# Two attention layers on one core: scores multiplied into the projection weights, F and G merged, the raw path moved behind the projection

## What is computed

```python
# layer 0: linear attention on qkv and on a depthwise 5x5 + grouped 1x1 copy of qkv
q, k, v = h @ wq.T, h @ wk.T, h @ wv.T
qkv = concat(q, k, v)                                  # 768 channels
pw = grouped_1x1(depthwise_5x5(qkv))                   # 768 channels
f = concat(qkv, pw).reshape(B, -1, 24, N)              # 32 "raw" and 32 "pw" heads
query, key_, value = relu(f[:, :, :8]), relu(f[:, :, 8:16]), f[:, :, 16:]
scores = einsum('bhdn,bhen->bhde', concat(value, 1), key_)
out = einsum('bhde,bhen->bhdn', scores, query)
out = out[:, :, :-1] / (out[:, :, -1:] + 1e-15)
x = batchnorm(conv1x1(out, proj)) + x
# layer 1: softmax attention over the 1024 pixels
norm = (x - mean(x)) / sqrt(var(x) + 1e-5)             # per channel
F, G = f_w @ norm + f_b, g_w @ norm + g_b
attention = softmax(F.T @ G)
x = o_w @ ((h_w @ x + h_b) @ attention.T) + o_b + x
```

## Time and profile before

| | us |
|---|---|
| median of 3 runs | 808.69 |
| lowest to highest | 807.97 to 808.84 |
| the profiled execution, its own time | 805.62 |
| its span, first to last instruction | 803.8 |
| busy: PE, DVE, POOL, ACT | 679.6, 597.0, 538.6, 505.5 |

### The profile page before, as it was taken

One profiled execution on the slowest core, in us unless ns is written; L12 is line 12 of the kernel. 1 busy time (PEld: TensorE's weight loads), 2 busy tenths in 40 slices (PEclk: granted clock), 3 DMA queues, 4 the chain that ended last, 5 costly groups with the idle time before them and its releaser, 6 DMA issues.

```text
span 803.8 us, 9440 instructions
## 1 busy us (share of the span) xinstructions
PE 679.6 (85%) x2892; PEld 457.7 (57%) x2892; DVE 597.0 (74%) x769; ACT 505.5 (63%) x731; POOL 538.6 (67%) x248
## 2 busy tenths in 40 slices
PE   4999988897788799898688799898688794888987
PEld 3744577655465477665465477665465462456743
DVE  6999599989757879989757879989757885443300
ACT  4944468865679768865679768865679754123730
POOL 3498968898778688997778688997778667000000
PEclk9999999999899999999899999999899997999999
DMA  5000020000000220000000220000000020000000
GB/s 200 2 0 1 0 106 1 1 1 0 1 1 1 79 79 0 0 0 0 0 0 0 79 79 0 0 0 0 0 0 0 27 79 0 1 0 1 1 26 26
DMA packets 4801, 15.93 MB, mean 20 GB/s; under 512 B 672, under 2 KB 928, under 8 KB 3744
## 3 DMA queue, kind: packets, MB, share of 16 engines
q1 hardware_dynamic: 4768, 15.56, 5.3%
HBM read 11.37 MB, written 4.19 MB: 19 GB/s over the span
## 4 chain that ended last, share of the span: by engine, by line
PE 48%; DVE 20%; ACT 13%; issue 13%; POOL 3%; DMA 1%; ACTq 0%; DVEq 0%; SPq 0%; POOLq 0%
PE ps L568 14%; DVE ps L937 9%; PE ps L494 7%; PE ps L544 6%; ACT prod L748 3%; PE ps L622 3%; PE ps L451 3%; PE ps L447 3%; PE ps L448 3%; POOL rows L1160 3%; PE ps L517 2%; ACT rows L862 2%; PE ps L504 2%; PE ps L559 2%; ACT kv L878 2%
## 5 line engine op out<-in xcount | busy, mean ns | idle before, releaser
L1160 POOL TENSOR_TENSOR conv<-conv,prod 128x930 f32<-128x930 f32 (+4 forms) x192 | 429.5, 2271 | 101.3 <-ACT prod L748 97.6
L937 DVE SCALAR_TENSOR_TENSOR ps<-raw,dw_sb,ps 128x960 f32<-128x960 f32 (+4 forms) x290 | 348.4, 1201 | 12.7 <-issue 4.8
L748 ACT ACTIVATE prod<-raw,dw_sb 128x930 f32<-128x930 f32 (+4 forms) x228 | 249.7, 1120 | 75.1 <-POOL conv L1160 62.4
L568 PE MATMUL ps<-kv,oc 128*128 128x512 f32 x256 | 111.6, 594 | 2.7 <-ACT kv L878 2.7
L1160 POOL TENSOR_TENSOR rows<-rows,prod 128x930 f32<-128x930 f32 (+4 forms) x36 | 83.2, 2310 | 14.9 <-ACT prod L748 12.3
L568 PEld LDWEIGHTS ps<-kv,oc 128*128 128x128 f32 x256 | 48.3, 190 | 61.4 <-issue 57.4
L1090 DVE TENSOR_REDUCE small<-ps 128x1 f32<-128x1024 f32 x32 | 39.2, 1225 | 58.1 <-PE ps L544 58.1
L559 PE MATMUL ps<-mask_sb,rows 128*128 128x128 f32 x256 | 37.6, 289 | 30.4 <-ACT kv L878 21.4
L517 PE MATMUL ps<-sd,rows 128*128 128x144 f32 x256 | 48.1, 322 | 17.7 <-DVE kv L999 13.7
L622 PE MATMUL ps<-oc,proj_sb 128*128 128x512 f32 x128 | 56.0, 595 | 1.4 <-ACT oc L774 0.8
L517 PEld LDWEIGHTS ps<-sd,rows 128*128 128x128 f32 x256 | 36.9, 201 | 31.0 <-DVE kv L999 23.5
(11 more groups left out here) (96 smaller groups left out, 1135.6 us busy)
## 6 DMA issues: line engine op xcount, KB each, us to landing
rows<-x_dram SPq DMA_DIRECT2D x4, 1024.0 KB, 4.9
x<-x_dram SPq DMA_DIRECT2D x4, 1024.0 KB, 4.8
out_dram<-x SPq DMA_DIRECT2D x8, 512.0 KB, 3.1
conv<-wqkv_dram SPq DMA_DIRECT2D x1, 768.0 KB, 4.4
conv<-fg_dram SPq DMA_DIRECT2D x1, 512.0 KB, 5.5
proj_sb<-proj_dram SPq DMA_DIRECT2D x1, 512.0 KB, 7.2
pw_sb<-pw_dram SPq DMA_DIRECT2D x1, 384.0 KB, 6.5
conv<-hw_dram SPq DMA_DIRECT2D x1, 256.0 KB, 5.7
```

The lines of the kernel that those rows point to most:

```text
L568: mm = pe.matmul(ps[:, 4 + c, :], ht[:, j, c * P:(c + 1) * P], pt[:, j, :], start=(j == 0), stop=(j == NB - 1))
L748: act.activation(dst, view, ACT.Copy, scale=weight(t, i)).then_inc(prod_ready, 1)
L937: return dve.scalar_tensor_tensor(dst, view, w, before, ALU.mult, ALU.add)
L1160: pool.tensor_tensor(total, total, product, ALU.add).then_inc(conv_pool, 1)
```

## The change

- **Scores into the weights.** The masked scores of both paths (`s_masked`) are transposed on TensorE (`score_transposes`, into `s_t`) and multiplied into the projection weights (`fused_weights`, into `mb`). The projection then takes `mb` and the scaled queries. The output matmuls, their eight-block division and the transposes back are gone.
- **q scaled by inverse denominators.** `denominators` multiplies q by `kd` (the key sums) with 32 output rows for each quarter of the pixels, so that all denominators of a path stand in one 128 x 256 block; VectorE adds epsilon and inverts it once; `spread_denominators` multiplies it by a 0/1 matrix with 32 contracted rows to copy each head's value to its channels; VectorE multiplies q by that, in four units of 512 pixels (`scaled_queries`). Before the second half of each pair of units TensorE waits for its own first half (`bc_part`).
- **F and G merged.** F.T @ G = norm.T (f_w.T g_w) norm and terms of the biases. `fg_hi` and `fg_lo` hold f_w.T g_w, made in the prologue; in a body only t = (merged weight) norm is made, four units in place of eight. The bias terms of a row come from 16 matmuls with one column each (`row`), and each row's maximum gets one more tiny VectorE operation with them.
- **Order.** Pointwise q comes straight behind the pw scores; the transposes of the next keys and values stand behind the denominators. The next image's q, its denominators, fused weights and scaling stand behind the projection: on VectorE its denominators before `normalise`, its scaling before the low part of the norm.
- **Memory.** x, its high and low parts, the norm's, raw q and `ht` have buffers of their own; the next x is loaded and split earlier (in the prologue, and at the end of each body for the body after next); `PROD_BUFS` is 4 in place of 3.
- **Loops and tables.** All four bodies are unrolled; all filler tables are new.

```diff
-PROD_BUFS = 3
+PROD_BUFS = 4
-CARRY = 16
+CARRY = 15
...
-TAPS_SCORES_PW, TAPS_OUTPUTS_PW, TAPS_SCORES_RAW, TAPS_OUTPUTS_RAW = 10, 7, 0, 2
-TAPS_PROJ = (3, 2, 0)
-TAPS_STATS = (1, 1)
-TAPS_NORM = (2, 1)
-TAPS_FG = (0, 0, 1, 1, 2, 1, 1, 1)
-TAPS_ATT = (1, 1, 2, 2, 2, 2, 0, 9, 3)
-TAPS_FINAL = (9, 8)
...
-LATES_PWKV = (1, 1, 0, 1, 0, 0, 0, 1)
-LATES_RAWKV = (1, 1, 1, 2, 1, 2, 0, 2)
-PRODUCTS_PWQ = 5
-PRODUCTS_RAWQ = (0, 2, 1, 1)
...
-PRODUCTS_FG = (1, 1, 1, 0, 3, 0, 1, 1)
-PRODUCTS_ATT = (1, 1, 1, 1, 1, 0, 7, 0)
-PRODUCTS_END = (1, 1, 1, 1, 1, 1, 0, 0, 0, 1)
+TAPS_SCORES_PW, TAPS_DEN_PW, TAPS_OUT_PW, TAPS_SCORES_RAW = 6, 4, 5, 0
+TAPS_PROJ = (4, 3, 3)
+TAPS_STATS = (0, 3)
+TAPS_NORM = (1, 0)
+TAPS_OUT_RAW = 0
+TAPS_T = (3, 1, 1, 0)
+TAPS_ATT = (3, 2, 2, 2, 2, 3, 2, 7, 0)
+TAPS_FINAL = (17, 12)
...
+PRODUCTS_KVT = (2, 1, 0, 0, 0, 0, 1, 1, 1)
+LATES_PWKV = (2, 0, 0, 1, 1, 0, 0, 0)
+LATES_RAWKV = (4, 0, 0, 5, 3, 5, 0, 5)
+PRODUCTS_PWQ = 3
+PRODUCTS_RAWQ = (1, 1, 0, 3)
+PRODUCTS_PROJ = 8
+PRODUCTS_HT = (2, 1, 1, 0)
+PRODUCTS_T = (0, 2, 0, 7)
+PRODUCTS_ATT = (1, 0, 0, 1, 1, 1, 10, 0)
+PRODUCTS_END = (0, 1, 1, 1, 0, 0, 0, 0, 0, 2)
...
+            def denominators(slot, scores_slot, q, q_done):
+                pe.wait_ge(d_free, scores_slot + 1)
+                pe.wait_ge(a_free, q_done)
+                dst = d_slot(slot)
+                for h in range(CK):
+                    for g in range(QUARTERS):
+                        mm = pe.matmul(dst[HEADS * g:HEADS * (g + 1), 0:QUARTER], kd[:, HEADS * h:HEADS * (h + 1)],
+                                       q[:, h, g * QUARTER:(g + 1) * QUARTER], start=(h == 0), stop=(h == CK - 1))
+                mm.then_inc(d_full, 1)
...
+            def spread_denominators(slot, dens):
+                pe.wait_ge(den_ready, dens)
+                for h in range(CK):
+                    banks = [d_slot(slot + 2 * h + i) for i in range(2)]
+                    for i in range(2):
+                        if i == 1:
+                            pe.wait_ge(bc_part, CK * (dens - 1) + h + 1)
+                        for half in range(2):
+                            g = 2 * half + i
+                            mm = pe.matmul(banks[half][:, i * QUARTER:(i + 1) * QUARTER],
+                                           head_rows[HEADS * g:HEADS * (g + 1), h, :],
+                                           den[HEADS * g:HEADS * (g + 1), :], start=True, stop=True)
+                        if i == 0:
+                            mm.then_inc(bc_part, 1)
+                    mm.then_inc(d_full, 2)
...
-                outputs(d0 + do["out_pw"], do["out_pw"], a0 + ao["pwq"] + A_PWQ)
+                score_transposes(A_AT["st_pw", b], D_AT["sc_pw", b])
+                denominators(D_AT["den_pw", b], D_AT["sc_pw", b], qp, A_AT["pwq", b] + A_PWQ)
                 if with_next:
-                    raw_qkv(b + 1, a0 + ao["raw_q"], ao["raw_q"], Q_TILES)
-                    scores(d0 + do["sc_raw"], do["sc_raw"], a0 + ao["kvt"] + A_KVT, RB)
-                out_transposes(a0 + ao["tr_pw"], ao["tr_pw"], d0 + do["out_pw"] + D_OUT)
+                    kv_transposes(b + 1)
+                fused_weights(A_AT["mb_pw", b], A_AT["st_pw", b], 1)
+                spread_denominators(D_AT["bc_pw", b], 2 * b + 2)
                 if with_next:
-                    outputs(d0 + do["out_raw"], do["out_raw"], a0 + ao["raw_q"] + A_RAWQ)
...
+                    scores(D_AT["sc_raw", b + 1], A_AT["kvt", b + 1] + A_KVT, RB)
...
                 if with_next:
-                    out_transposes(a0 + ao["tr_raw"], ao["tr_raw"], d0 + do["out_raw"] + D_OUT)
+                    score_transposes(A_AT["st_raw", b + 1], D_AT["sc_raw", b + 1])
+                    raw_qkv(b + 1, A_AT["raw_q", b + 1], Q_TILES)
+                    denominators(D_AT["den_raw", b + 1], D_AT["sc_raw", b + 1], qr, A_AT["raw_q", b + 1] + A_RAWQ)
...
+                if with_next:
+                    fused_weights(A_AT["mb_raw", b + 1], A_AT["st_raw", b + 1], 0)
+                    spread_denominators(D_AT["bc_raw", b + 1], 2 * b + 3)
...
+                dve.tensor_scalar(den[:], d_bank(slot)[:, 0:QUARTER], ATT_EPS, None, ALU.add).then_inc(d_free, 1)
+                dve.wait_ge(d_free, slot + 1)
+                dve.reciprocal(den[:], den[:]).then_inc(den_ready, 1)
...
+                    dve.tensor_tensor(q[:, t, cols], q[:, t, cols], d_bank(slot + u), ALU.mult).then_inc(d_free, 1)
```

733 lines of the change are left out of this document (367 added, 366 removed).

## The result

The changed kernel takes **823.2 us** (819.5 to 825.0, four runs), the kernel before 808.8 in the same job: a ratio of 1.017 (95% interval 1.013 to 1.021). It is slower. The forecast of 773 was wrong in sign, and the time lies outside its range, 748 to 798.

The account below looks back on a forecast made before the run. Hand-overs between engines, more than one full engine, were taken to bound the kernel. From 805.6, three steady bodies gave -25.5 and the last -9.8: 770.3, forecast as 773 us, range 748 to 798.

Parts of the forecast that it names:

- Ledgers: Work per engine in a steady body: TensorE 20.1 us in, 21.5 out; VectorE 4.5 less; no engine forced above 150.
- rival 1: Narrow matmul tiles run side by side, so stages one and two lose more time: 748 to 760 us, chance 0.21.
- Stage one: Body start to first projection matmul: projection starts at T+48.5 instead of T+62.7, 14 us earlier.
- the row term (3.6) lies under that wait: Stage two, projection to first energy: 3.6 us of one-column bias matmuls hidden while VectorE's low part is late.
- The wait that I named as the one this change adds: Stage two: the norm's low part queues behind the raw query scalings until T+88.2, takes 6.6 us, ends T+94.8.
- The middle price's 3 us: Stage two: narrow matmuls at a middle price bring the first energy from T+104 to T+101.
- covered: Stage two: VectorE could start the norm's low part at T+79, hidden behind the scalings that end at T+88.2.
- Attention: Stage three of a steady body: grows from 69.9 to 71.6 us.
- rival 3: Slower: products bunched ahead of drains wait for POOL, a body of 188, 820 us in all; chance 0.09.
- Rival 2: POOL becomes the bound, bodies stay at 181 if it keeps its pauses: 786 to 800 us, chance 0.19.
- Ahead of body 0: Prologue: added work and savings cancel, 0 us taken, from -4 to +4.
- Last body: Body without a next one: 9.8 us less, from earlier F and G work against eight row corrections.

Follow-up runs that it names:

- the filled runs: Changed kernel plus idle 512-column matmuls where TensorE waited: in both stages 839.6 us, ratio 1.034; in stage one's spreading alone 830.8 us, ratio 1.022.
- the other order: Changed kernel with the diagonal convolution split, so that scores, denominators and spreading run beside it ahead of body 0: 813.9 us, ratio 1.008.
- the first combination: Changed kernel with raw spreading late, GpSimd paused for the normalisations and the first filler tables of the kernel before: 807.3 us, ratio 0.994.
- the best kernel: Changed kernel with late raw spreading, GpSimd paused until the low part is written, another order ahead of body 0 and stage-one idle matmuls: 780.4 us, ratio 0.964.

## Why the prediction was wrong

Of the 54.7 us between the -35.3 forecast and the +19.4 of the profiled executions, 13.1 lie ahead of body 0, 18.1 in body 0, 17.1 in bodies 1 and 2, and 6.4 in the last. T is the body's start, as in the prediction.

**Ledgers: right.** VectorE lost 6.0 us a body (4.5 forecast), POOL 1.7, and TensorE's matmuls hardly changed. The argument "no engine is forced, the gain has to come from order" was right, and order is where it failed.

**Prices.** The 256-column reciprocal is 1.75 (1.8 estimated), a scaling 0.64 to 0.69 (0.75). Eight denominator matmuls take 1.07 at 2.4 GHz and 1.94 at 1.2, near the lower end of 0.9; I took 2.2. The eight spreading matmuls of a path take two groups of 1.47 at the high clock (2.6 taken for both), with 1.5 of waiting between; in the steady bodies the second group ran at the low one, 2.50. So rival 1 was right in its premise and wrong in its time: what the cheap tiles gave was used up elsewhere on the chain, as the next two paragraphs show.

**Stage one: mechanism right, 3.8 short** (52.3 against 48.5). 2.8 of it is the clock, as the filled runs show: the raw scores at 5.92 instead of 4.26, the spreading's second half at 2.50 instead of 1.46. What the cheap denominators gave (1.07 for 3.5), the key transposes used up: 8.2 us for the 4.4 I had, 2.4 of it waiting for ScalarE's copies. I priced all matmuls at the high clock, though the earlier trace rows had 0.89 in the one thin stage, and the change made a second thin stage.

**Stage two: the step that failed is "the row term (3.6) lies under that wait".** The low part ended at T+94.8, to the tenth of a microsecond as forecast, by luck: it started 3.0 late, at T+91.2, and took 3.59 where I had 6.6. The row term waited for the spreading as well, started only 0.4 us ahead of the low part, took 6.96 at the low clock and ended 3.0 behind it; the t products then began at the low level. From the low part's end to the first energy it took 15.2 us, where I had 9.2. Leaving the row term out gave 4.5 of these 6. The wait that I named as the one this change adds was the right one, and taking it away gave 7 us, of which 4.5 are this same overlap; its price was what I set too low.

**The middle price's 3 us** off stage two were a second fault. TensorE came to the raw denominators at T+74.0, where I had T+70.5, since stage one ran 3.8 late, and ended the first spreading at T+86.0 (T+83.7 by whole matmuls). VectorE's pair, which I had let stand as "covered" at its old 2.8, took 5.1 and ended at the same moment. With POOL paused it took 1.53 and the first scaling still came at T+86.1 in body 1, so there the pair alone cost nothing.

**Contention: the section was read for the wrong instructions.** I used that section of the Trainium skill (SBUF — State Buffer, Who interferes with whom) for the scalings, which behaved as it says (1.28 a pair beside running adds). It bears as much on the normalisations, which I left out of the sum. That cost 8.4 in body 0 (13.48 against 5.1), and a wait for one add each would not have given it. The longest such row of before was 6.57, and the range had no case beyond it.

**Attention: right** (70.7 against 71.6), and rival 3 with it fell: no backlog stood ahead of the first exponential. That the kernel got slower, as rival 3 had it, came by other ways. Rival 2 had bodies of 181, and bodies of 181 came, with POOL idle for 35.5 us in them; but POOL was not the bound, since leaving out the row term shortened them by 3.3 and 4.0 with POOL's work unchanged.

**Ahead of body 0: 0 forecast, +13.1.** The diagonal convolution began 7 us later, and the longer chain behind it ran with nothing beside it, its spreading at 2.5 a half. TensorE before, then after:

```profile
36.66 6.32 PE L494 MATMUL ps<-raw,conv 128*128 128x512 f32 x16 [1.17 <-ACT raw L717]
...
43.71 6.31 PE L467 MATMUL ps<-raw,conv 128*128 128x512 f32 x16 [3.19 <-ACT raw L729]
...
111.17 0.69 PE L485 MATMUL ps<-mask_sb,s_masked 128*128 128x128 f32 x2 [7.13 <-DVE kd L988]
```

I had put the added matmuls there at two or three microseconds and their chain at +1, without asking what VectorE and ScalarE had queued; the other order took 9.5 off its end.

**Last body: -9.8 forecast, -3.4.** The first energy came 6.4 sooner, not 11.4, and the row loop grew 3.0 instead of 1.6. Of the missing 5.0, 1.4 lie ahead of the projection, 1.4 in the row term's end (counted from the projection, 2.4 behind the old start of F and G, where I had 1), and 2.1 from there to the first energy (9.3 for 7.2).

**Open**: what makes VectorE's pair take 5.1 or 14 beside such a row of adds. Its first operation started 0.34 to 0.46 us into an add where the pair took 5, 0.54 to 1.07 into one before the long waits, and 1.65 in the kernel before; but low parts that started 0.9 into an add (in the first combination) took turns, so this alone does not tell. Open too: why body 0's projection comes at 52, 54 or 57.5 in traces of kernels with no edit ahead of it, and why the attention grows by 2 to 6 us when the first energy comes sooner (its clock in the best kernel is 0.91 against 0.98 in the earlier trace rows; that this is the whole cause was not tried).

## What to carry to other kernels

Where work moves into a thin stage, ask of each queue what the critical result now stands behind, and give the moved part the latest place its consumer allows: the raw queries' scaling was needed only at the next projection, some 140 us later, and with that placement the median was 23 us lower (11 of it seen in the trace). Price the matmuls in thin stages at the low clock, and count waits, and one-column matmuls, among what it fell behind here. A gain in one place can move an engine into another's way: the fills cost 6 to 7 us a body until GpSimd's pause was in, and gave 14 us in all afterwards, so test such edits together as well as alone. And a pause only pays if nobody else then waits for the engine that paused: here ScalarE's products did, ahead of drains on the chain.

## What the hardware showed

VectorE's SBUF-to-SBUF operations met GpSimd's back-to-back adds in two ways. Taking turns: each operation waited for one add, the next add took 2.70 to 2.75 instead of 2.2 to 2.3, and a pair of 1.53 us took 5.1. Or shut out: one operation was held for the rest of a row of six adds (13.3 us), none of them over 2.31 in the changed kernel, and the pair took 13.5 to 14.0. A shift of the pair by 2.7 us in the body went with the change from one to the other.

The 32 records of one-column matmuls (16 matmuls, eight result columns) take 3.63 us at the high clock and 6.96 at the low. Eight matmuls that fill 32 of 128 output rows each take 1.07 (1.94 at the low clock), where eight whole ones would take 3.5 (0.44 each, from the earlier trace rows). Eight idle matmuls (1.45 and 0.97 us), put where TensorE waited, brought 2.8 us of stage one back: its granted clock went from 0.90 to 0.97.
